# A two-layer transformer-like step: weights laid out transposed on the host side of the call, split in place, and a reordered first chunk

## What is computed

```python
# layer 0
w   = weight * (mask, summed over 32x32 blocks, > 0)   # 512 x 512
s   = xn @ w.T + bias
inter = xn @ c1_w.T @ c2_w.T                            # 1792 wide, rank 16
idx = argmax within each segment of 32 of inter         # 56 winners a row
h   = relu(xn . w1[idx]);  f = sum h * w2t[idx]
# layer 1
s   = attention(xn, Wqkv, bqkv) @ Wo + bo               # one head of 128
f   = xn @ base_w.T + base_b + 0.5 * top-2-of-16 expert LoRA(xn; A, B, router_w)
```

## Time and profile before

| | |
|---|---|
| median of three runs | 699.52 us (699.08 to 701.77) |
| span of the profiled execution | 697.0 us |
| TensorE busy, instructions | 671.0 us (96%), 3220 matmuls |
| VectorE, ScalarE, GpSimd busy | 457.7, 208.3, 204.2 us |
| TensorE's granted clock | 1.00 of full speed in every slice until the end |
| moved by DMA | 40.25 MB, mean 58 GB/s |

### The profile page before, as it was taken

How to read it: one execution, slowest core, us unless ns; L and a number is a source line. 1 busy time by engine, 2 the same in 40 slices (tenths; PEclk the granted TensorE clock), 3 DMA queues, 4 the chain that set the end, 5 groups by cost and what they waited for, 6 DMA issues and landing times.

```text
span 697.0 us, 9078 instructions
## 1 busy us (share of the span) xinstructions
PE 671.0 (96%) x3220; PEld 529.0 (76%) x3220; DVE 457.7 (66%) x741; ACT 208.3 (30%) x371; POOL 204.2 (29%) x175
## 2 busy tenths in 40 slices
PE   4989999999999999999999999889999999999997
PEld 3867777777777777787777787667877887787787
DVE  8798664596765596665686656684855566485543
ACT  2621222412122312222311132563136115313610
POOL 3299100360000550000630003624424242442441
PEclk9999999999999999999999999999999999999999
DMA  8563000040000040000150004530021013002001
GB/s 273 188 189 111 14 1 0 23 159 0 0 0 0 31 149 0 0 0 0 45 197 1 0 1 122 121 136 1 30 91 62 0 46 135 0 30 90 1 15 46
DMA packets 30570, 40.25 MB, mean 58 GB/s; under 512 B 11888, under 2 KB 12656, under 8 KB 30544
## 3 DMA queue, kind: packets, MB, share of 16 engines
q1 hardware_dynamic: 30544, 39.90, 17.5%
HBM read 31.51 MB, written 8.39 MB: 57 GB/s over the span
## 4 chain that ended last, share of the span: by engine, by line
PE 83%; DVE 9%; issue 4%; DMA 1%; ACT 1%; POOL 1%; SPq 0%; DVEq 0%; POOLq 0%
PE bank L376 73%; DVE eq L916 2%; DVE seg_top L914 2%; PE bank L1201 2%; PE bank L314 2%; DVE counts L926 2%; PE bank L1297 2%; DMA s_tile<-in_L_attn_weight 1%; PE bank L1182 1%; PE bank L1334 1%; PE bank L1162 1%; POOL s_tile L639 1%; DVE h_lo L953 1%; DVE w1T_lo L522 1%; DVE x_tile L354 0%
## 5 line engine op out<-in xcount | busy, mean ns | idle before, releaser
L737 ACT ACTIVATE h_hi<-h 128x512 fp32r<-128x512 f32 x56 | 35.4, 632 | 206.6 <-DVE h L944 206.6
L376 PE MATMUL bank<-w_hi_t,h_hi 128*128 128x512 f32 x224 | 93.6, 418 | 0.8 <-DVE h_lo L953 0.6
L914 DVE TENSOR_REDUCE seg_top<-bank 128x16 f32<-128x512 f32 (+1 forms) x64 | 39.5, 617 | 77.2 <-PE bank L1182 77.2
L376 PE MATMUL bank<-xT_hi,w1T_hi 128*128 128x512 f32 x224 | 88.7, 396 | 0.0
L376 PE MATMUL bank<-w_hi_t,h_lo 128*128 128x512 f32 x224 | 88.5, 395 | 0.0
L376 PE MATMUL bank<-w_lo_t,h_hi 128*128 128x512 f32 x224 | 88.5, 395 | 0.0
L376 PE MATMUL bank<-xT_hi,w1T_lo 128*128 128x512 f32 x224 | 88.5, 395 | 0.0
L376 PE MATMUL bank<-xT_lo,w1T_hi 128*128 128x512 f32 x224 | 88.4, 395 | 0.0
L926 DVE TENSOR_TENSOR_SCAN counts<-restart,eq 128x512 bf16<-128x512 bf16 (+1 forms) x64 | 82.1, 1283 | 2.0
L346 POOL TENSOR_TENSOR rstd<-mean_var,eps 128x4 f32<-128x4 f32 x8 | 1.6, 203 | 271.9 <-DVE mean_var L340 271.9
L360 POOL TENSOR_TENSOR g_tile<-g_tile,s_tile 128x512 f32<-128x512 f32 x31 | 40.6, 1311 | 104.9 <-DVE g_tile L970 66.1
(11 more groups left out here) (201 smaller groups left out, 1327.4 us busy)
## 6 DMA issues: line engine op xcount, KB each, us to landing
x_res<-in_L_attn_data SPq DMA_DIRECT2D x4, 1024.0 KB, 7.6
mid_state<-g_tile SPq DMA_DIRECT2D x16, 256.0 KB, 2.1
x_tile<-mid_state SPq DMA_DIRECT2D x4, 1024.0 KB, 7.5
x_res<-mid_state SPq DMA_DIRECT2D x4, 1024.0 KB, 5.5
out<-g_tile SPq DMA_DIRECT2D x15, 256.0 KB, 2.0
x_tile<-in_L_attn_data SPq DMA_DIRECT2D x3, 1024.0 KB, 5.4
g_tile<-in_L_ffn_w SPq DMA_DIRECT2D x8, 256.0 KB, 5.4
g_tile<-in_L_ffn_w2t SPq DMA_DIRECT2D x8, 256.0 KB, 3.7
```

The source lines that it names most:

```text
L376: last = nc.tensor.matmul(dst, a, b, start=(start and n == 0), stop=(stop and n == len(mms) - 1))
L737: nc.scalar.activation(h_hi[:, it % 2, :], h[:], ACT.Copy).then_inc(h_hi_done, 1)
L914: nc.vector.reduce_max(seg_top[:, 0:segs], got, AX.X).then_inc(seg_max, 1)
```

## The change

`kernel()` lays the weights out with numpy before the launch: transposed, and in the order in which the partitions hold them. The kernel loads them straight into place, and all weight transposes go from TensorE. Each matrix's raw values land where its `_lo` part will be (`raw_at`), ScalarE rounds them from there, and GpSimd subtracts in place (`w1_rest`, `w2_rest`), without staging places and without waits on loads' places. The mask multiply and the subtraction for ws are now VectorE's. c2 is loaded four times, to four groups of partitions.

In the first chunk x is loaded first, its rows are normalized and transposed ahead of all else, the mask is counted behind that, and TensorE does the first two `up_product` ahead of the `s_product`, whose four results go to the banks of `down_product`. ScalarE rounds two slices (w1 four rounds ahead, w2 two) in each round of the first chunk's body, which for that is written out apart from the loop. Layer 1's weights are loaded and split during layer 0's last chunk: wqkv and A with router_w from round 4 on, base_w and Wo in rounds 7 and 8, B in rounds 10 to 13, the subtractions all on GpSimd (`next_layer`, `next_b`).

```diff
--- before
+++ after
...
+        span_1h = Span(max(span_s.end, next_s.end))
+        w1_hi_t = span_1h.take("w1_hi_t", [P, IT, KD, P], F32R)
+        span_1l = Span(span_1h.end)
+        w1_raw = raw_at("w1_raw", [P, IT, KD, P], span_1l.end)
+        w1_lo_t = span_1l.take("w1_lo_t", [P, IT, KD, P], F32R)
...
+            for q in range(2):
+                sp.dma_start(x_tile[:, 2 * q:2 * q + 2, :], x_rows[0][:, 2 * q:2 * q + 2, :])\
+                    .then_inc(ld_x if q else ld_x_first, 16)
+                if q == 0:
+                    sp.dma_start(c1_nat[:], c1_w).then_inc(ld_c1, 16)
+            sp.dma_start(mask_nat[:], mask).then_inc(ld_mask, 16)
+            sp.wait_ge(c2_zero, 1)
+            for q in range(4):
+                sp.dma_start(c2_f[q * Q:q * Q + RANK, :], c2_w).then_inc(ld_c2, 16)
+            sp.dma_start(w1_raw[:, 0], w1[0]).then_inc(ld_w1[0], 16)
+            sp.dma_start(ws_raw[:], w_s0).then_inc(ld_ws0, 16)
+            sp.dma_start(w1_raw[:, 1], w1[1]).then_inc(ld_w1[1], 16)
+            for it in range(2, IT + 2):
+                if it < IT:
+                    sp.dma_start(w1_raw[:, it], w1[it]).then_inc(ld_w1[it], 16)
+                sp.dma_start(w2_raw[:, it - 2], w2[it - 2]).then_inc(ld_w2[it - 2], 16)
...
-                sp.wait_ge(w2_lo, IT)
-                sp.wait_ge(c2_wide, 1)
                 sp.dma_start(x_res[:], x_rows[c]).then_inc(ld_res, 16)
...
 
-                    sp.wait_ge(up_done, CH * IT)
-                    sp.dma_start(base_nat[:], base_w.rearrange("(t p) k -> p t k", p=P)).then_inc(ld_base, 16)
-                    sp.dma_start(wo_nat[:], wo).then_inc(ld_base, 16)
-                    for t in range(TT):
-                        sp.dma_start(b_nat[:, t], lora_b[:, rows(t), :].rearrange("e p r -> p e r")).then_inc(ld_b, 16)
+                    sp.wait_ge(up_done, (CH - 1) * IT + KD + 1)
+                    sp.dma_start(base_raw[:], base_w).then_inc(ld_base, 16)
+                    sp.dma_start(wo_raw[:], wo).then_inc(ld_base, 16)
+                    for i in range(2):
+                        part = slice(i * KE // 2, (i + 1) * KE // 2)
...
-            gp.wait_ge(mask_on, 1)
-            gp.wait_ge(ld_ws0, 16)
-            for t in range(TT):
-                part = ws_nat[:, t, :].rearrange("p (n s) -> p n s", s=SEG)
-                nc.gpsimd.tensor_tensor(part, part, on[:, t * MB:(t + 1) * MB][:, :, None].to_broadcast([P, MB, SEG]),
-                                        ALU.mult).then_inc(ws0_masked, 1)
+            def w1_rest(it):
+
+                gp.wait_ge(w1_hi, it + 1)
+                nc.gpsimd.tensor_tensor(w1_lo_t[:, it], w1_raw[:, it], w1_hi_t[:, it].bitcast(F32), ALU.subtract).then_inc(w1_lo, 1)
+
...
+            w1_rest(0)
+            w1_rest(1)
+            for it in range(2, IT + 2):
+                if it < IT:
+                    w1_rest(it)
+                w2_rest(it - 2)
...
+                nc.gpsimd.tensor_tensor(wqkv_lo[:], wqkv_raw[:], wqkv_hi[:].bitcast(F32),
+                                        ALU.subtract).then_inc(wqkv_split, 1)
+                nc.gpsimd.tensor_tensor(a_lo[:], a_raw[:], a_hi[:].bitcast(F32),
+                                        ALU.subtract).then_inc(wqkv_split, 1)
...
+                    gp.wait_ge(base_hi_done, k + 1)
+                    nc.gpsimd.tensor_tensor(base_lo[:, k, :], base_raw[:, k, :], base_hi[:, k, :].bitcast(F32),
+                                            ALU.subtract).then_inc(base_split, 1)
+                gp.wait_ge(base_hi_done, KD + 1)
+                nc.gpsimd.tensor_tensor(wo_lo[:], wo_raw[:], wo_hi[:].bitcast(F32),
+                                        ALU.subtract).then_inc(base_split, 1)
+
+            def next_b():
+
+                for k in range(KE):
+                    gp.wait_ge(b_hi_done, k + 1)
+                    nc.gpsimd.tensor_tensor(b_lo[:, k, :], b_raw[:, k, :], b_hi[:, k, :].bitcast(F32),
+                                            ALU.subtract).then_inc(b_split, 1)
+
...
+                if last:
+                    next_layer()
                 rows_rstd(gp, c + 1)
                 if last:
-
-
...
+            def next_layer(it):
+
+                if it == 4:
+                    act.wait_ge(ld_wqkv, 2 * 16)
+                    nc.scalar.activation(wqkv_hi[:], wqkv_raw[:], ACT.Copy).then_inc(wqkv_hi_done, 1)
+                    nc.scalar.activation(a_hi[:], a_raw[:], ACT.Copy).then_inc(wqkv_hi_done, 1)
...
+                    nc.scalar.activation(wo_hi[:], wo_raw[:], ACT.Copy).then_inc(base_hi_done, 1)
+                if it >= IT - 4:
+                    i = it - (IT - 4)
+                    act.wait_ge(ld_b[i // 2], 16)
...
+                    if first:
+                        if it == 0:
+                            for k in range(KD):
+                                act.wait_ge(ws0_masked, k + 1)
+                                nc.scalar.activation(ws_hi[:, k, :], ws_raw[:, k, :], ACT.Copy).then_inc(ws_hi_done, 1)
+                            w1_round(2)
+                            w2_round(0)
+                            w1_round(3)
+                            w2_round(1)
+                            for tt in range(TT):
+                                s_read(c, tt)
+                        if it + 4 < IT:
+                            w1_round(it + 4)
+                        if it + 2 < IT:
+                            w2_round(it + 2)
+                    if last:
+                        next_layer(it)
                     act.wait_ge(h_masked, c * IT + it + 1)
                     if it >= 2:
...
+            rows_norm(dve, 0)
...
+            c2_rest(0)
             t_rest(0)
...
-            with dve.Fori(0, CH - 1) as c:
+            dve.wait_ge(mask_cnt, 1)
+            nc.vector.tensor_scalar(on[:, 0:KD * MB], mask_bank[:, 0:KD * MB], 0.0, None, ALU.is_gt).then_inc(mask_on, 1)
+            dve.wait_ge(mask_on, 1)
+            dve.wait_ge(ld_ws0, 16)
+            for k in range(KD):
+                part = ws_raw[:, k, :].rearrange("p (n s) -> p n s", s=SEG)
+                nc.vector.tensor_tensor(part, part, on[:, k * MB:(k + 1) * MB][:, :, None].to_broadcast([P, MB, SEG]),
+                                        ALU.mult).then_inc(ws0_masked, 1)
+            c2_rest(1)
+            for k in range(KD):
+                dve.wait_ge(ws_hi_done, k + 1)
+                nc.vector.tensor_tensor(ws_lo[:, k, :], ws_raw[:, k, :], ws_hi[:, k, :].bitcast(F32),
+                                        ALU.subtract).then_inc(ws_split, 1)
+            dve.wait_ge(c2_split, 2)
+            for tt in range(TT - 1):
+                select(0, 0, tt)
+            body(0, False)
+            head(1)
+            with dve.Fori(1, CH - 1) as c:
...
+            pe.wait_ge(mask_sum, 1)
+            nc.tensor.matmul(mask_bank[:, 0:KD * MB], seg_ones, row_cnt[:, 0:KD * MB],
+                             start=True, stop=True).then_inc(mask_cnt, 1)
+            up_product(0, 0, True)
+            pe.wait_ge(c2_split, 1)
+            select(0, 0, 0)
+            up_product(0, 1, True)
+            pe.wait_ge(ws_split, KD)
             for tt in range(TT):
-                s_product(0, tt)
-                if tt:
-                    select(0, 0, tt - 1)
-                for n in AFTER_S[tt]:
-                    item_in(pe, n)
-            with pe.Fori(0, CH - 1) as c:
+                s_product(0, tt, True)
+                if tt < TT - 1:
+                    select(0, 0, tt + 1)
+            pe.wait_ge(c2_split, 2)
+            body(0, True)
...
+                if is_first:
+                    pe.wait_ge(wqkv_split, 2)
...
                 for j, dst in enumerate((pj[1], sc[0], sc[1])):
+                    if is_first and j == 1:
+                        pe.wait_ge(silu_done, CH * TT)
...
                         three(dst[:], parts[3:], start=False).then_inc(proj_done, 1)
-                    if is_first:
-                        if j == 0:
-                            pe.wait_ge(silu_done, CH * TT)
-                            pe.wait_ge(pick_ready, 4)
-                        for n in LATE_GROUPS[j]:
...
+                    pe.wait_ge(base_split, KD + 1)
+                    pe.wait_ge(pick_ready, 4)
...
+    a_w = np.concatenate([np.asarray(inputs["L1_ffn_A"]), np.asarray(inputs["L1_ffn_router_w"])])
+    laid = {
+        "x": x,
+        "mask": by_k(np.asarray(inputs["L0_attn_mask"])),
+        "w_s0": by_k(np.asarray(inputs["L0_attn_weight"])),
+        "b_s0": np.asarray(inputs["L0_attn_bias"]),
+        "c1_w": by_k(np.asarray(inputs["L0_ffn_c1_w"])),
+        "c2_w": np.asarray(inputs["L0_ffn_c2_w"]).T,
+        "w1": w1.reshape(IT, P, KD, P).transpose(0, 3, 2, 1),
+        "w2": w2.reshape(IT, P, D),
```

563 lines of the change are left out of this document (210 added, 353 removed).

## The result

The changed kernel takes 693.81 us (median of 4 runs, 692.08 to 694.31) against 700.28 us of the kernel before (4 runs, 699.08 to 701.77): a ratio of 0.990, 95% interval 0.988 to 0.992. The profiled executions have spans of 692.2 and 697.0 us. It is faster, as forecast, but by 6.5 us (4.8 in the spans) and not by 12, and the time lies 0.8 us above the range. In every run on record, of either kernel, the time is 1.75 to 1.97 us above the span of the same execution. So some 0.6 of the 2.5 us that the prediction put around the span came from setting a median beside the span of a faster execution.

The account below looks back on a forecast made before the run. TensorE, 83% of the chain that ended last, was taken to bound the kernel. First chunk -4.0, fourth +0.3 and layer 1's first -8.3 gave -12.0: span 685.0, time 687.5 us, range 680 to 693.

Parts of the forecast that it names:

- step 4: Layer 0's fourth chunk: loses 2.3 us of excess, gains GpSimd's turns (wqkv 1.5, base, Wo and B 1.1): +0.3 us.
- step 5: Layer 1's first chunk: transposes and their waits go, 2.6 us of GpSimd's turns in the routing stay: -8.3 us.
- step 2: Opening up to the s products: GpSimd's turns delay ws, s starts at 30.8 us, TensorE idles 6.7, clock costs 2.0.
- Step 1: Ahead of the first rank product: norms start earlier, rows are ready at 15.7 us, rank product starts 4.2 us earlier.
- Step 3: Rest of the first chunk: 93.1 us plus clock, rounds and root; second rank product at 127.4 us, -4.0 us.
- the late items: In layer 1's first routing: three subtractions of late items and their waits, 2.4 us, which the change removes.
- Rival A: Opening: no GpSimd turns at ws and no clock fall; s starts at 27.5, time 681.0 us; chance 0.22.
- B: Turns bind the whole first body: first chunk gains nothing, fourth loses 2, layer 1 gains 7.5; 694.0 us; chance 0.15.
- C: Idle time ahead of the s products drops the clock to half pace and it stays: 710 us; chance 0.03.
- the stricter reading: At ws: the shared ports lock for a whole instruction, so four turns instead of three; s starts at 31.9 us.

Follow-up runs that it names:

- 6: The changed kernel with 48 transposes of the identity, which nobody reads, ahead of the first row transposes: 693.69 us, ratio 0.991.
- 4: The changed kernel with GpSimd's subtractions of w1 from slice 2 on held until VectorE has done the four of ws: 689.57 us, ratio 0.984.
- 1: The changed kernel with GpSimd's eight closing operations of layer 0's last chunk held back until layer 1's first routing is done: 691.87 us, ratio 0.988.
- 2: The changed kernel with ScalarE's roundings of B placed behind `h_hi` instead of ahead of it: 692.54 us, ratio 0.990.
- 5: The changed kernel with 24 matmuls nobody reads ahead of the s products, to keep TensorE busy: 693.44 us, ratio 0.991.
- 8: The changed kernel with wqkv's subtraction in four pieces and B's subtractions moved behind GpSimd's closing operations: 696.22 us, ratio 0.994.
- 9: The changed kernel with wqkv's subtraction in four pieces, B rounded earlier and four of its subtractions ahead of the reciprocal root: 688.27 us, ratio 0.982.
- 3: The changed kernel with GpSimd's 1536-wide subtraction of wqkv cut into four of 384: 692.51 us, ratio 0.987.
- 7: The changed kernel with layer 0's last closing operations held behind the routing, those of tiles 2 and 3 behind the fourth and sixth `prod_lo`: 688.32 us.
- 11: 10 with VectorE's subtraction of c2's second part moved behind the four of ws: 677.17 us, ratio 0.968.
- 10: The changed kernel with the moves of 3, 4, 7 and 9 together, only the order of GpSimd's instructions changed: 678.78 us, ratio 0.970.

## Why the prediction was off

The direction, the places and the mechanism (GpSimd's turns) were right. What failed is the size of steps 4 and 5, whose losses were put too small, and one length in step 2. Of the 7.2 us between the forecast span (685.0) and the measured one (692.2), steps 1 to 3 have 1.4, step 4 has 2.3 and step 5 has 3.5.

- **Step 1** (-4.2, rows ready at 15.7). Rank product at 16.41. The norms started at 10.57, 0.2 late, and all sixteen row transposes were at half pace (3.65 us; in 6 the first twelve took 1.57), and so the last rows came 0.7 late.
- **Step 2** (s at 30.8, clock 2.0). The mechanism is confirmed by 4: four subtractions of ws took 5.70 with three of GpSimd's between them, where I had 2.8 + 3.3, and 2.50 without. The start was 32.35 because the rank product ran at half pace, 3.77 us for my 2.1. In the first executions of 1 and 2, which differ only behind this point, it ran at full pace, and the s products started at 30.34 and 30.50; in the second of 2 it ran at half pace, and they started at 33.24. The clock's fall cost 2.7 us in the profile of after (5.5 for 12 matmuls that later take 2.8) and 2.2 by 5. That it would fall was right. Rival A fails twice: the turns came, and in 4, where they are gone and the s products start at A's 27.5 (27.34), the clock fell even so.
- **Step 3** (second rank product at 127.4). 128.84 in the profile of after; 126.3 and 126.4 in 1 and 2. My number lies between the two openings. From the first s product to the second rank product my terms gave 96.6 (93.1 + 2.0 + 1.0 + 0.5), and 96.5 was measured; without the clock's fall they gave 94.6, and 5 has 94.0. So the 1.4 us that steps 1 to 3 missed all came ahead of the s products. No run isolated the ten rounds.
- **Step 4** (+0.3). It failed: +2.6. Without the turns the -2.3 would have come (102.5 in 8 and 9), and wqkv cost the 1.5 that I took (3). But B cost 3.0 where I put 1.1 (8, 9): I had called its turns "mostly in slack" and counted one of eight, while TensorE's waits for x_tile and xT_lo, 1.8 us before, grew by 1.0 and did not go. Another 0.35 is over the undisturbed length in 8 and 9 too; that it is the pick table beside an h_lo was not tried. The total is beyond my bound of +2.4.
- **Step 5** (-8.3). -4.8, the term that weighs most. The routing took 9.0 us, against 4.8 in 1: 4.2 of turns, where I had read 2.6 out of the earlier trace rows by giving the late items the rest. The five operations from 446.50 to 452.24 are longer than in 1 by 0.3, 0.75, 1.1, 0.9 and 1.1. So TensorE waited 3.3 and not 1.3. The longer wait also dropped the clock, which the sum has no term for: three matmuls, the transposes and three matmuls took 3.5 us for 1.8 in 7. 3.3 + 1.7 are 5.0 of the 5.1 us between 66.2 and 61.1; -9.9 was to be had.
- **Rivals.** The time landed at B's (694.0), but not by B: it had the first chunk gain nothing, and that chunk gained 2.5 us or more. Its 2 us in the fourth chunk did come, its 7.5 in layer 1 did not. What I gave for it was also read too strongly: the earlier trace rows has 0.5 us lost in two rounds, 0.25 a round and not 0.5. C (half pace stays) is refuted: full pace came back after some dozen matmuls at most in every profile on record. The danger that ScalarE's roundings make `h_hi` late cost nothing that 2 could find.

The Trainium skill, "SBUF — State Buffer" (section "Who interferes with whom"), says that an instruction of VectorE with two inputs in SBUF contends with one of GpSimd that reads SBUF, and that one with at most one input there, outside VectorE's 2-port modes, does not. The trace agrees: 1.31 us for the former, 0.22 for the maximum at 447.05 inside one of GpSimd's. I had used the page only for ws. Had I counted the routing's steps by it, the five that met a closing operation would have made 5.5 us at the 1.1 a turn of step 2, where I had 2.6 and 4.2 was measured; that it would be five I know from the trace of after. The four turns at ws of the stricter reading in step 2 did not come in the profile of after, where three lay between, but in 6 they did: ws_lo took 6.65 us beside four of GpSimd's.

The Trainium skill, "TensorE: Matmul & The Clock Gate" (section "Part 1: The HAM clock gate"), says that a TensorE left idle goes back to 1.2 GHz. The traces agree for each wait of 2.7 us and more, behind which matmuls stood 0.43 us apart; behind the 1.9 us of 1 they did so in one execution and not in the other. It would not have mended step 5 by itself: after waits of 1.1 and 1.7 us the clock stayed, so the 1.3 us of wait that I had there asked for no such term, and the 3.3 us did.

## What to carry to other kernels

When work goes from TensorE to GpSimd, don't ask whether GpSimd has time, but which short chain of VectorE runs at that moment, and count a turn of GpSimd for each of its operations with two inputs in SBUF. Hold GpSimd back by a wait on what VectorE has finished, in pieces, with what is needed first in front; here that was worth 15 us, more than twice the change itself. And put the clock's price on every new wait of TensorE of the size behind which it fell here (each of 2.7 us and more, and 1.9 us in one of two executions): that was 1.6 us (the two executions of 1) to 2.7 us (the twelve matmuls of after).

## What the runs showed of the hardware

- Whichever comes second waits for the other's end. A scan that began 0.42 us behind GpSimd's 3.51 took 4.16 instead of 1.22, and the two last steps of the routing in 8 took 2.40 instead of 0.36. The other way round, a subtraction of GpSimd that began in 11 just behind VectorE's 1.48 us for c2 took 2.59 instead of 1.29. Beside ws it took 1.6 to 1.72.
- The clock fell after waits of 2.7 (4, 10), 3.3, 5.8 and 6.9 us (after, 6) and stayed after waits of 1.1 (11) and 1.7 (the fourth chunk of after). After the 1.9 us of 1 it fell in one execution and stayed in the other. In 1 and 4 it fell only when TensorE was at work again, for 1.5 and 0.8 us. The same wait of 3.3 us cost five slow matmuls in after, eleven in 5 and twelve in the second execution of 2.
- The same opening came out in two ways: the rank product's first matmul at 0.77 us (after, 3, 5, 8, 9) or at 0.47 (1, 2, 4, 7, 10, 11). It goes with the execution and not with the kernel: in the second executions 2 has 0.76 and 128.87 for the second rank product, and 3 has 0.47 and 126.46. Where nothing else differed, the second rank product stood at 128.5 to 129.0 (after, 3, 8, 9) or at 126.3 to 127.3 (1, 2, 7). One profile can't tell an effect of that size at the start; stages cut at their own starts agreed to 0.3 us, but for the clock's falls, which moved layer 1's first chunk by up to 1.6 us between two executions of one kernel (1: 64.7 and 63.1).
- The clock column stands at 1.00 in the opening of after, where matmuls ran at half pace: 0.43 us from start to start tells what the column doesn't.
